# Scatter of expert rows by token, loads of 120 rows, and unread products between turned tiles

## The chip, the cores and the metric

The kernel runs on one core of one Trainium2 chip. The metric is the device time of one execution in microseconds (us). Kernels are compared by the median of several executions.

## The reference

The reference is a graph network of two layers over 1250 nodes with 768 features and 40,000 weighted edges. Layer 0 has two graph attention layers, linear attention and a mixture of experts, and its end is where the change lies. For each node a gate picks 2 of 8 experts. The node's row goes through both, and the two results are added with the gate's weights:

```python
h = jax.nn.relu(dispatched @ W1[e] + b1[e])
expert_outputs = expert_outputs + sel * (h @ W2[e] + b2[e])
...
rerouted = jnp.zeros((S * K, m), expert_outputs.dtype).at[dispatch_mask].set(expert_outputs)
combined = jnp.einsum('ks,ksm->sm', combine_weights, rerouted.reshape(K, S, m))
```

The combined rows are added to the residual and normalised (mean and variance over 768 features). Layer 1 begins with a low-rank adapter, relu(x Wd + bd) with 24 columns and then Wu, and a graph convolution with a 768x256 weight; linear attention and a spline layer follow. All of it is float32.

## The kernel before, in words

The nodes lie in 10 tiles of 125 rows. `acc` holds the residual, tile by tile, with a node to a partition. The order of instructions on each engine is written out by hand: each engine's program is a loop or a straight list, and semaphores tie them. PSUM is a ring of 4 slots of two banks, and `packets` is the list that says in which order the slots are taken. A slot is free once the packet 4 places earlier has been copied out.

Dispatch. A node's row of `xf` is scattered to two slots of `xs_rows` in HBM (POOL, indirect DMA), so that the rows of an expert lie together. SP then loads 27 tiles of 128 rows (`dispatched`, L654), and TensorE turns a tile (L1189), multiplies it by the expert's W1 (L1200) and W2 (L1211). VectorE copies the result to one of three buffers `yb` (L2309), and POOL writes it to `y_rows` in the same order of slots (L836).

Combine. When all of `y_rows` is written, POOL gathers for each tile of nodes 125 rows for the first expert and 125 for the second (L842, an indirect DMA each, 20 in all, into `back[k][t]`). For each tile VectorE adds share times row twice (L2328), then takes the statistics (L1832, L1834, L1835). ScalarE takes the root (L1417, `root_of`), VectorE the reciprocal and the negated mean times it (L2312, L2313, `lowered`), ScalarE writes the normalised tile to `H` (L1583, `normalised`). TensorE turns it with 6 transposes (L1238, packet `T x3`), and ScalarE copies the turned tile to `xT` (L1375, `turned_tile`).

Adapter. Its first product has two halves of the nodes, `down(0)` and `down(1)` (L955, packets `ad 0` and `ad 1`); ScalarE applies the relu (`low_rank`). `down(0)` stands after the seventh turned tile, `down(1)` after the tenth. Then TensorE forms the convolution's features (L1253, L1255, packets `cg`) and, with a weight that SP loads back from HBM when the tenth tile is normalised (`WA`, two loads at L551 from `spill_w`), the convolution itself (L1264).

## Time and profile before

| | |
|---|---|
| median of 3 runs | 2820.5 us |
| lowest, highest | 2816.82, 2822.02 us |
| the profiled execution | 2820.71 us |
| its span | 2819.0 us |
| mean granted clock of TensorE | 0.979 |
| PE busy | 2686.1 us (95%) |
| DVE busy | 1481.2 us (53%) |
| ACT busy | 889.0 us (32%) |
| POOL busy | 100.9 us (4%) |

The trace has PE for TensorE, PEld for its weight loads, DVE for VectorE, ACT for ScalarE, POOL for GpSimd, SP for the engine that issues most DMAs. Busy time says how much an engine ran, and not what ended a stage; for that the stretch between the last expert tile and the convolution has to be read alone. The expert loop runs from about 1195 to 1431 us of the span, the combine stage from 1431 to 1500 us, and `cg` begins at 1500.13 us.

### The profile page before, as it was taken

How to read it: one execution, taken by the hardware profiler on the slowest of the kernel's cores; microseconds unless marked ns; L12 is line 12 of the kernel's file. 1: busy time of each engine (PE TensorE's matmuls, PEld its weight loads, DVE VectorE, ACT ScalarE, POOL GpSimd, SP SyncE). 2: the span in 40 equal slices, each digit the busy share in tenths (PEclk: the TensorE clock that was granted, in tenths of full speed). 3: DMA queues.
4: the chain of work that ended last, by engine and by line, in shares of the span. 5: the costliest groups of instructions: out<-in, count | busy, mean ns of one | idle time of the engine just before them, and what ended most of it. 6: DMA issues, size and time to landing. Idle time of an engine off the chain costs nothing.

```text
span 2819.0 us, 30928 instructions
## 1 busy us (share of the span) xinstructions
PE 2686.1 (95%) x11845; PEld 1862.8 (66%) x11845; DVE 1481.2 (53%) x2298; ACT 889.0 (32%) x1528; POOL 100.9 (4%) x144
## 2 busy tenths in 40 slices
PE   6999999899989999899959999999999999999999
PEld 5786656698976556577736755566677776555555
DVE  7897899699962555511151210244877774331230
ACT  8895101244421332222221211032644442311210
POOL 1000000000000001100040000000000000000000
PEclk9999999999999999899969999999999999999999
DMA  9904222211030301499946111000200013000000
GB/s 236 334 5 92 96 65 70 72 72 38 19 72 28 73 12 53 139 386 359 358 138 136 39 34 34 0 15 1 90 30 30 30 34 130 6 11 6 11 11 11
DMA packets 131739, 238.12 MB, mean 84 GB/s; under 512 B 18639, under 2 KB 99572, under 8 KB 131118
## 3 DMA queue, kind: packets, MB, share of 16 engines
q1 hardware_dynamic: 116418, 192.97, 22.3%
q0 software_dynamic: 15200, 43.44, 4.6%
q8 instruction: 87, 1.43, 0.2%
q14 instruction: 34, 0.28, 0.0%
HBM read 173.10 MB, written 63.25 MB: 84 GB/s over the span
## 4 chain that ended last, share of the span: by engine, by line
PE 84%; DVE 9%; DMA 3%; ACT 1%; issue 1%; DVEq 1%; POOL 0%; SPq 0%; POOLq 0%; ACTq 0%
PE ps L938 22%; PE ps L1363 15%; PE ps L1320 14%; PE ps L1152 5%; PE ps L955 4%; PE ps L892 4%; PE ps L1062 4%; PE ps L1211 4%; PE ps L1200 4%; PE ps L1264 2%; DVE arena L1990 1%; DVE arena L1983 1%; DVE arena L1798 1%; PE ps L1253 1%; DMA arena<-in_x_dram 1%
## 5 line engine op out<-in xcount | busy, mean ns | idle before, releaser
L938 PE MATMUL ps<-arena 128*125 128x384 f32 x2112 | 697.1, 490 | 6.8 <-DVE arena L1909 2.7
L938 PEld LDWEIGHTS ps<-arena 128*125 128x125 f32 x2112 | 396.1, 189 | 284.3 <-issue 13.8
L1363 PE MATMUL ps<-arena 128*125 128x384 f32 x1280 | 415.4, 488 | 5.8 <-DVE arena L2395 5.8
L1320 PE MATMUL ps<-arena 128*128 128x312 f32 (+1 forms) x1536 | 407.1, 427 | 5.7 <-DVE arena L2395 5.7
L1320 PEld LDWEIGHTS ps<-arena 128*128 128x128 f32 x1536 | 291.6, 190 | 120.0 <-issue 6.6
L1363 PEld LDWEIGHTS ps<-arena 128*125 128x125 f32 x1280 | 241.3, 189 | 179.8 <-issue 8.5
L2395 DVE SCALAR_TENSOR_TENSOR arena<-arena 128x1250 f32<-128x1250 f32 (+3 forms) x175 | 232.0, 1347 | 93.9 <-PE ps L1320 91.6
L1375 ACT ACTIVATE arena<-ps 128x750 f32<-128x750 f32 (+6 forms) x140 | 108.1, 777 | 509.8 <-PE ps L938 201.2
L892 PE MATMUL ps<-arena 128*125 128x380 bf16 x1280 | 213.4, 328 | 11.1 <-DVE arena L1798 11.0
L1909 DVE SCALAR_TENSOR_TENSOR arena<-ps,arena 125x768 f32<-125x768 f32 x30 | 28.7, 955 | 346.9 <-PE ps L1363 292.9
L892 PEld LDWEIGHTS ps<-arena 128*125 128x125 bf16 x1280 | 173.0, 137 | 51.2 <-DVE arena L1798 14.0
L1391 ACT ACTIVATE arena<-arena 128x125 bf16<-128x125 bf16 x640 | 189.6, 386 | 34.0 <-DVE arena L1788 34.0
L1062 PE MATMUL ps<-arena 125*125 125x97 f32 x1600 | 179.0, 273 | 5.1 <-DVE arena L1990 5.1
L1062 PEld LDWEIGHTS ps<-arena 125*125 125x125 f32 x1600 | 177.7, 189 | 7.8 <-DVE arena L1990 4.2
L1968 DVE CUSTOM_DVE_ANT_0 arena<-arena 125x1250 bf16<-125x1250 bf16 x90 | 131.3, 1459 | 25.5 <-DMA arena<-al_src 22.9
L955 PE MATMUL ps<-arena 128*128 128x312 f32 (+5 forms) x496 | 138.1, 438 | 4.4 <-DVE arena L1938 2.4
L1152 PE MATMUL ps<-arena 125*125 125x385 f32 (+1 forms) x400 | 135.5, 494 | 2.8 <-DVE arena L2195 2.8
L2309 DVE COPY arena<-ps 128x768 f32<-128x768 f32 x27 | 25.8, 957 | 208.6 <-PE ps L1211 208.6
L1482 ACT ACTIVATE arena<-arena,small 125x1250 f32<-125x1250 f32 x80 | 105.2, 1333 | 71.3 <-DVE arena L1983 71.3
L1983 DVE SCALAR_TENSOR_TENSOR arena<-arena,small 125x1250 f32<-125x1250 f32 x80 | 120.8, 1512 | 2.8 <-DMA arena<-al_dst 2.8
L955 PEld LDWEIGHTS ps<-arena 128*128 128x128 f32 (+2 forms) x496 | 89.7, 183 | 47.7 <-issue 15.1
L1200 PEld LDWEIGHTS ps<-arena 128*128 128x128 f32 x972 | 112.7, 192 | 8.0 <-issue 1.2
(321 smaller groups left out, 2538.1 us busy)
## 6 DMA issues: line engine op xcount, KB each, us to landing
arena<-in_L_ffn_W_dram SPq DMA_DIRECT2D x54, 1152.0 KB, 7.8
xs_rows<-arena SPq DMA_DIRECT2D x1, 30720.0 KB, 99.5
arena<-in_kw_dram SPq DMA_DIRECT2D x24, 512.0 KB, 4.7
arena<-al_dst POOLq DMA_DIRECT2D x18, 625.0 KB, 4.9
arena<-xs_rows SPq DMA_DIRECT2D x27, 384.0 KB, 7.5
y_rows<-arena POOLq DMA_DIRECT2D x27, 384.0 KB, 6.5
arena<-in_kw_dram SPq DMA_DIRECT2D x6, 1536.0 KB, 10.0
arena<-in_x_dram SPq DMA_DIRECT2D x2, 3600.0 KB
```

Of the source, the lines that this page charges most:

```text
L892: mm = pe.matmul(bank(s, min(k, 1)), oh_src[:, par, u, k, :], oh_spot[:, par, u, :], start=(fresh and u == 0 and k < 2), stop=False, skip_ ...
L938: mm = pe.matmul(slot(g)[0:TILE, 512 * half:512 * half + HALF], xt[:, k, i * TILE:i * TILE + TILE], w[:, k, :], start=(k == 0), stop=(k == ...
L955: mm = pe.matmul(slot(g)[0:rows, 512 * b:512 * b + w], stat, mov[:, lo + b * w:lo + b * w + w], start=(t == 0), stop=(t == len(terms) - 1))
L1062: mm = pe.matmul(slot(g)[0:TILE, 512 * (j // 5) + 97 * (j % 5):512 * (j // 5) + 97 * (j % 5) + 97], AT[m % AHEAD][:, j * TILE:j * TILE + T ...
L1152: mm = pe.matmul(slot(g)[0:TILE, 512 * b:512 * b + w], AT2[i][:, j * TILE:j * TILE + TILE], H769[:, i, lo:lo + w], start=(i == 0), stop=(i ...
L1200: mm = pe.matmul(slot(g)[:, 0:TAU], w1s[t % ERING][:, k, f * P:f * P + P], xsT[t % 2][:, k, :], start=(k == 0), stop=(k == KT - 1))
L1320: mm = pe.matmul(slot(g)[:, 512 * b:512 * b + wd_], w[:, r % 2, ORDER[p], o * P:o * P + P], feat[place(f)][:, lo + b * wd_:lo + b * wd_ + ...
L1363: mm = pe.matmul(slot(g)[0:TILE, 512 * b:512 * b + HALF], fv[:, q, :], w2c[m][q][:, b * HALF:b * HALF + HALF], start=(p == 0 and q == 0), ...
L1391: ins = act.activation(oh_src[:, par, u, 1 + k, :], oh_src[:, par, u, 0, :], ACT.Copy, scale=w_p[k][:, bass.ds(col + u, 1)])
L1968: chain(dve.tensor_tensor_reduce(out=scratch, in0=neg[:, j, :], in1=row[0:TILE], scale=1.0, scalar=-3.0e38, op0=ALU.add, op1=ALU.max, accu ...
L1983: dve.scalar_tensor_tensor(out=AT[m % AHEAD], in0=d[0][0:TILE], scalar=alD[:, i, h:h + 1], in1=d[1][0:TILE], op0=ALU.add, op1=ALU.max).the ...
L2395: return dve.scalar_tensor_tensor(out=out_, in0=in_, scalar=edge, in1=of, op0=op, op1=ALU.mult)
```

## The change

The expert result now goes straight to its node, and several things follow from it.

1. A row of `xs_rows` has 770 words: the 768 features, the node's number plus one, and its first slot. The zero fill ahead covers 10,368 such rows. `slots` has one copy more.
2. In the expert loop VectorE works out, for each of the 128 rows of a tile, where its result belongs (`destination`, four small operations), and POOL scatters the tile by an indirect DMA to `z_rows`: rows 1 to 1250 the results for the first expert by node, the next 1250 those for the second, and spare rows behind. SP's load of tile t also waits until `destination` is done for tile t-3.
3. When all of `z_rows` is written, SP loads it: first rows 120 to 124 of all ten tiles, one load of 5 partitions for each expert (`back_rest`), then rows 0 to 119, 20 loads of 120 rows. The 20 gathers on POOL are gone.
4. VectorE's second addition gives the row's sum as well (`accum_out`). The squares are summed by ScalarE (`squares`, with the negated mean as bias), and VectorE's statistics are gone. The table for the root is loaded ahead (`primed`).
5. `low_rank(0)` stands behind the tenth turned tile instead of the seventh, and a tile is turned out one step later on ScalarE.
6. TensorE forms products of the identity with itself that nothing reads (`unread`): 40 behind the product for `F`, and 11 behind each of the first six turned tiles. Each set takes a slot of the ring.

```diff
+    packet("spin", NT)
     for i in range(NT):
         packet("T", "x3", i)
+        if i < 6:
+            packet("spin", i)
         if i == 6:
             packet("ad", 0)
...
+ROW = 768 + 2
+        xs_d = nc.dram_tensor("xs_rows", (EXP * ROOM + TAU, ROW), F32).ap()
+        z_d = nc.dram_tensor("z_rows", (1 + 2 * NODES + NTAU * TAU, D), F32).ap()
...
             def dispatched(t):
                 if t >= ERING:
                     sp.wait_ge(packet_ready, packets["sT", t - ERING] + 1)
+                    sp.wait_ge(ev("dest"), t - ERING + 1)
...
+            for q in range(3):
+                sp.wait_ge(ev(f"y_out{q}"), 16 * len(range(q, NTAU, 3)))
+            for k in range(2):
+                load(back_all[k][120:TILE], rows_z[k][120:TILE], "back_rest")
+            for t in range(NT):
+                for k in range(2):
+                    load(back[k][t][0:120], rows_z[k][0:120, t, :], f"back{t}")
...
             for n in range(NTAU):
                 emptied(pool, "so", n)
-                pool.dma_start(y_d[n * P:n * P + P], yb[n % 3]).then_inc(ev(f"y_out{n % 3}"), 16)
+                pool.wait_ge(ev("dest"), n + 1)
+                pool.indirect_dma_start(out=z_d, out_offset=bass.IndirectOffsetOnAxis(ap=desti[:, n:n + 1], axis=0),
+                                        in_=yb[n % 3], in_offset=None).then_inc(ev(f"y_out{n % 3}"), 16)
...
-                    pool.indirect_dma_start(out=back[k][t], out_offset=None, in_=y_d,
-                                            in_offset=bass.IndirectOffsetOnAxis(ap=ysloti[:, k, t:t + 1], axis=0))\
...
+            unread(NT, 40)
             for i in range(NT):
                 turn("x3", i, H)
                 if i == 6:
                     down(0)
+                elif i < 6:
+                    unread(i, 11)
             down(1)
...
+            def squares(i):
+                act.wait_ge(ev("centred"), i + 1)
+                act.activation(H[:, i, :], acc[:, i, :], ACT.Square, bias=nmu[:, i:i + 1], accum_out=ssq[:, i:i + 1])\
+                   .then_inc(ev("squared"), 1)
...
-            normalised(0)
-            for i in range(NT):
-                if i + 1 < NT:
-                    normalised(i + 1)
-                turned_tile("x3", i, xT)
-                if i == 6:
-                    act.wait_ge(ev("u_ones"), 1)
-                    low_rank(0)
+            own.step(act.activation(primed, onesc, ACT.Sqrt))
+            for i in range(NT):
+                squares(i)
+                root_of(i)
+                if i >= 1:
+                    turned_tile("x3", i - 1, xT)
+                normalised(i)
+            turned_tile("x3", NT - 1, xT)
+            act.wait_ge(ev("u_ones"), 1)
+            low_rank(0)
             low_rank(1)
...
+            def destination(n):
+                dve.wait_ge(ev(f"xs_{n % ERING}"), 16 * (n // ERING + 1))
+                own.step(dve.tensor_scalar(home[:, 0:1], first, rowp[:, n:n + 1], float(NODES), ALU.not_equal, ALU.mult))
+                chain(dve.tensor_scalar(home[:, 1:2], token, 0.0, spare[:, n:n + 1], ALU.is_equal, ALU.mult))
+                chain(dve.scalar_tensor_tensor(out=home[:, 0:1], in0=home[:, 0:1], scalar=home[:, 1:2], in1=token,
+                                               op0=ALU.add, op1=ALU.add))
+                dve.tensor_copy(desti[:, n:n + 1], home[:, 0:1]).then_inc(ev("dest"), 1)
...
+            dve.wait_ge(ev("back_rest"), 32)
             for t in range(NT):
                 dve.wait_ge(ev(f"back{t}"), 32)
...
+                own.step(dve.scalar_tensor_tensor(out=acc[:, t, :], in0=back[0][t], scalar=share[:, 0, t:t + 1],
+                                                  in1=acc[:, t, :], op0=ALU.mult, op1=ALU.add))
+                if t >= 1:
+                    varied(t - 1)
+                own.settle()
+                chain(dve.scalar_tensor_tensor(out=acc[:, t, :], in0=back[1][t], scalar=share[:, 1, t:t + 1],
+                                               in1=acc[:, t, :], op0=ALU.mult, op1=ALU.add, accum_out=total[:, t:t + 1]))
                 if t >= 1:
-                    lowered(t - 1, counted[t - 1])
+                    lowered(t - 1)
+                dve.tensor_scalar(nmu[:, t:t + 1], total[:, t:t + 1], -1.0 / D, None, ALU.mult).then_inc(ev("centred"), 1)
```

SP's list of DMAs, between the small weights of layer 1 and the return of `WA` (`spill_w`). Before:

```order
L551 DMA arena<-in_L_gnn_Wd_dram 128x6x24
L551 DMA arena<-in_L_gnn_Wu_dram 24x768
L551 DMA arena<-in_L_gnn_W_dram 128x6x256
L551 DMA small<-in_L_gnn_b_dram 125x256
L551 DMA arena<-spill_w 120x12800
L551 DMA arena<-spill_w 5x12800
```

and after the change, where `load` is L564:

```order
L564 DMA arena<-in_L_gnn_W_dram 128x6x256
L564 DMA small<-in_L_gnn_b_dram 125x256
L564 DMA arena<-z_rows 5x10x768 x2
L564 DMA arena<-z_rows 120x768 x20
L564 DMA arena<-spill_w 120x12800
L564 DMA arena<-spill_w 5x12800
```

The two loads of 5 partitions and the twenty of 120 rows stand in one queue, ahead of the return of `WA`.

TensorE's list from the product for `F` (25x256) to the first `cg`. Before:

```order
L1224 MATMUL ps<-arena 25x256 x6
L1238 MATMUL ps<-small,arena 128x125 x42
L955 MATMUL ps<-arena 24x312 x12
L1238 MATMUL ps<-small,arena 128x125 x18
L955 MATMUL ps<-arena 24x313 x12
L1253 MATMUL ps<-arena 125x256 x6
```

and after the change the head of the same place, where the turn is L1271 and the unread products L952 and L954:

```order
L1257 MATMUL ps<-arena 25x256 x6
L952 MATMUL ps<-small 128x128
L954 MATMUL ps<-small 128x128 x39
L1271 MATMUL ps<-small,arena 128x125 x6
L952 MATMUL ps<-small 128x128
L954 MATMUL ps<-small 128x128 x10
L1271 MATMUL ps<-small,arena 128x125 x6
```

The 42 transposes of the first seven tiles stood in one run; now 11 products stand between each two of them, and 40 ahead of the first. `down(0)` and `down(1)` keep their places.

ScalarE's list at the head of the combine stage. Before:

```order
L1417 ACT_TABLE_LOAD
L1417 ACTIVATE small<-small 125x1
L1583 ACTIVATE arena<-arena,small 125x768
L1417 ACTIVATE small<-small 125x1
L1583 ACTIVATE arena<-arena,small 125x768
L1375 ACTIVATE arena<-ps 128x6x125
```

and after, where the squares are L1618, the root L1453, the normalised tile L1623 and the copy of the turned tile L1411:

```order
L1626 ACTIVATE arena<-small 128x1
L1618 ACTIVATE arena<-arena 125x768
L1453 ACTIVATE small<-small 125x1
L1623 ACTIVATE arena<-arena,small 125x768
L1618 ACTIVATE arena<-arena 125x768
L1453 ACTIVATE small<-small 125x1
L1411 ACTIVATE arena<-ps 128x6x125
L1623 ACTIVATE arena<-arena,small 125x768
```

The copy of turned tile i now stands ahead of the normalising of tile i+1, and behind its squares and root.

## Rows read from the trace of the kernel before

**Rows 1.** Chain of waits, 1425 to 1450 us: start, us, what.
```profile
1430.42 2.59 DMA y_rows<-arena
...
1434.05 1.26 POOL arena L842
...
1435.61 7.80 DMA arena<-y_rows,arena
...
1443.44 1.03 DVE arena L2328
```

**Rows 2.** Timeline of TensorE, 1425 to 1545 us: start, us, what [idle before <-releaser].
```profile
1424.76 4.11 PE L1211 MATMUL ps<-arena 128*128 128x384 f32 x12 [0.66 <-ACT arena L1375]
...
1430.48 2.77 PE L1224 MATMUL ps<-arena 128*25 128x256 f32 x12 [1.13 <-DVE small L2321]
1451.84 1.51 PE L1238 MATMUL ps<-small,arena 125*128 125x125 f32 x6 [18.59 <-ACT arena L1583]
...
1474.24 1.51 PE L1238 MATMUL ps<-small,arena 125*128 125x125 f32 x6 [2.22 <-ACT arena L1583]
1475.69 8.44 PE L955 MATMUL ps<-arena 128*24 128x312 f32 x24
1484.06 0.86 PE L1238 MATMUL ps<-small,arena 125*128 125x125 f32 x6
...
1490.76 9.44 PE L955 MATMUL ps<-arena 128*24 128x313 f32 x24 [1.09 <-ACT arena L1375]
1500.13 2.85 PE L1253 MATMUL ps<-arena 128*125 128x256 f32 x12
...
1535.15 4.55 PE L1264 MATMUL ps<-arena 125*125 125x256 f32 x20
```

**Rows 3.** Timeline of VectorE, the second tile of the combine stage.
```profile
1449.01 1.02 DVE L1832 BATCH_NORM_STATS2 small<-arena 125x6 f32<-125x384 f32 x2
...
1450.57 0.16 DVE L2313 SCALAR_TENSOR_TENSOR arena<-small 125x1 f32<-125x1 f32 x1
```

**Rows 4.** Timeline of ScalarE in the combine stage.
```profile
1450.76 1.03 ACT L1583 ACTIVATE arena<-arena,small 125x768 f32<-125x768 f32 x1 [3.53 <-DVE arena L2313]
...
1455.43 0.78 ACT L1375 ACTIVATE arena<-ps 128x750 f32<-128x750 f32 x1
...
1484.23 0.77 ACT L1375 ACTIVATE arena<-ps,small 24x624 f32<-24x624 f32 x1 [5.63 <-PE ps L955]
```

**Rows 5.** ScalarE's read of a sum, line L1618: ns, first to last start.
```profile
L1618 ACT ACTIVATION_READ_ACCUMULATOR arena<-ps x20: 194/194/195, 1663.2 to 1893.4; 125x1 f32 x20
```

**Rows 6.** Windows: PE, PEld, DVE, ACT, POOL, PEclk, DMA share, GB/s.
```profile
820.00:823.00 3.00, 3.00 (x11) 1.77 (x10) 0.00 (x0) 0.00 (x0) 0.00 (x0) 1.00 0.98 194
...
825.00:826.00 1.00, 1.00 (x4) 0.56 (x3) 0.00 (x0) 0.00 (x0) 0.00 (x0) 1.00 0.92 69
...
1195.00:1431.00 236.00, 234.05 (x1431) 184.94 (x1431) 26.72 (x32) 51.52 (x107) 14.68 (x27) 1.00 0.95 341
...
1460.00:1470.00 10.00, 3.84 (x16) 2.67 (x15) 9.52 (x24) 4.20 (x8) 8.65 (x6) 0.50 0.70 210
```

**Rows 7.** VectorE's first read of x, in the timeline.
```profile
830.01 0.96 DVE L1909 SCALAR_TENSOR_TENSOR arena<-ps,arena 125x768 f32<-125x768 f32 x1 [11.12 <-DMA arena<-in_x_dram]
```

**Rows 8.** POOL's DMA queue, 1040 to 1150 us (14 scatters).
```profile
q0 software_dynamic: 3136, 5.39, 17.7%
```

**Rows 9.** POOL's DMA queue, 1195 to 1429 us (26 stores).
```profile
q0 software_dynamic: 2080, 10.23, 10.6%
```

**Rows 10.** Expert loop, a tile: SP's issue and TensorE's turn two tiles on.
```profile
1201.59 0.77 SPq L654 DMA_DIRECT2D arena<-xs_rows  x1
...
1221.85 0.82 PE L1189 MATMUL ps<-small,arena 128*128 128x128 f32 x6
```

**Rows 11.** DMA issues of the page: KB each, us to landing.
```profile
arena<-xs_rows SPq DMA_DIRECT2D x27, 384.0 KB, 7.5
```

**Rows 12.** SP's return of WA, in the timeline.
```profile
1488.79 0.69 SPq L551 DMA_DIRECT2D arena<-spill_w  x2
```

More of the change, by code:

```diff
@@ L395, in build @@
         sloti = rcut(2 * NT)[0:TILE].bitcast(I32).rearrange("p (k t) -> p k t", k=2)
-        yslotf = rcut(2 * NT)[0:TILE].rearrange("p (k t) -> p k t", k=2)
-        ysloti = rcut(2 * NT)[0:TILE].bitcast(I32).rearrange("p (k t) -> p k t", k=2)
+        total = rcut(NT)[0:TILE]
+        ssq = rcut(NT)[0:TILE]
+        nmu = rcut(NT)[0:TILE]
+        ptab = rcut(1)
+        spare = rcut(NTAU)
+        home = rcut(2)
+        primed = rcut(1)
         share = rcut(2 * NT)[0:TILE].rearrange("p (k t) -> p k t", k=2)
@@ L420, in build @@
         assert ro[0] <= 4700
-        xf = ct_r[0:TILE, 0:NT * D].rearrange("p (t d) -> p t d", t=NT)
+        X0 = R_ACC + R_XT + R_CT - NT * ROW
+        xf_all = arena[0:TILE, X0:X0 + NT * ROW].rearrange("p (t d) -> p t d", t=NT)
+        xf = [xf_all[:, NT - 1 - t, :] for t in range(NT)]
         xfT = [aa_r[:, 750 * n:750 * n + 750].rearrange("p (k n) -> p k n", k=KT) for n in range(2)]
@@ L424, in build @@
         w2s = [r[:, 2304:4608].rearrange("p (k n) -> p k n", k=3) for r in (aa_r[:, 0:4608], aa_r[:, 4608:9216], h_r)]
-        xs2 = [aa_r[:, 9216 + D * n:9984 + D * n] for n in range(ERING)]
+        xs2 = [aa_r[:, 9216 + ROW * n:9216 + ROW * n + ROW] for n in range(ERING)]
         xsT = [ct_r[:, D * n:D * n + D].rearrange("p (k n) -> p k n", k=KT) for n in range(2)]
@@ L824, in _ @@
             own.step(pool.memset(b2m, 0.0))
+            pool.wait_ge(ev("A_in"), (HEADS + 1) * NT)
+            own.step(pool.iota(ptab, [[0, 1]], base=0, channel_multiplier=1,
+                               allow_small_or_imprecise_dtypes=True))
+            own.step(pool.iota(spare, [[TAU, NTAU]], base=1 + NODES, channel_multiplier=1,
+                               allow_small_or_imprecise_dtypes=True))
+            own.step(pool.iota(xf_all[:, :, D], [[-TILE, NT]], base=1 + (NT - 1) * TILE, channel_multiplier=1,
+                               allow_small_or_imprecise_dtypes=True))
             own.settle()
@@ L922, in _, with unread @@
             pe.wait_ge(ev("adj_all"), 1)
+            def unread(n, times):
+                g = take_slot("spin", n)
+                pe.matmul(slot(g)[:, 0:P], ident, ident, start=True, stop=True).then_inc(slot_free[packet_at[g][0]], 1)
+                for _ in range(times - 1):
+                    mm = pe.matmul(slot(g)[:, 0:P], ident, ident, start=True, stop=True)
+                ready(mm)
             def transposes(s, src, event):
@@ L2257, in _ @@
                 emptied(dve, "agg2", j)
-                normal("xf", j, statistics(j, acc), acc, xf)
+                normal("xf", j, statistics(j, acc), acc, xf[j][:, 0:D])
             slots(NT - 2)
@@ L2291, in _ @@
                 chain(dve.tensor_reduce(b1t[:, :, f], btmp, AXX, ALU.add))
-            chain(dve.scalar_tensor_tensor(out=posf, in0=begin[0:TILE].unsqueeze(1).broadcast_to([TILE, NT, EXP]),
-                                           scalar=float(TAU), in1=pref, op0=ALU.mult, op1=ALU.add))
-            for k in range(2):
-                chain(dve.scalar_tensor_tensor(out=ptmp, in0=rank, scalar=float(k), in1=posf, op0=ALU.is_equal,
-                                               op1=ALU.mult))
-                chain(dve.tensor_reduce(yslotf[:, k, :], ptmp, AXX, ALU.add))
-            chain(dve.tensor_copy(ysloti, yslotf))
             dve.tensor_copy(rz, dinv).then_inc(ev("b1t"), 1)
@@ L2323, in _ @@
             give(dve.tensor_copy(WF, slot(g)[0:RANK + 1, 0:HID]), g)
-            counted = []
+            dve.wait_ge(ev("back_rest"), 32)
             for t in range(NT):
                 dve.wait_ge(ev(f"back{t}"), 32)
-                for k in range(2):
-                    chain(dve.scalar_tensor_tensor(out=acc[:, t, :], in0=back[k][t], scalar=share[:, k, t:t + 1],
-                                                   in1=acc[:, t, :], op0=ALU.mult, op1=ALU.add))
-                counted.append(statistics(t, acc))
+                own.step(dve.scalar_tensor_tensor(out=acc[:, t, :], in0=back[0][t], scalar=share[:, 0, t:t + 1],
+                                                  in1=acc[:, t, :], op0=ALU.mult, op1=ALU.add))
                 if t >= 1:
-                    lowered(t - 1, counted[t - 1])
-            lowered(NT - 1, counted[NT - 1])
+                    varied(t - 1)
[5 more added lines that the diff above has]
+                dve.tensor_scalar(nmu[:, t:t + 1], total[:, t:t + 1], -1.0 / D, None, ALU.mult).then_inc(ev("centred"), 1)
+                dve.wait_ge(ev("centred"), t + 1)
+            varied(NT - 1)
+            chain(dve.tensor_scalar(mv[:, :, 1], ssq, 1.0 / D, None, ALU.mult))
+            lowered(NT - 1)
             hs = rq
@@ L2434, in _ @@
                 emptied(dve, "vo", i)
[L2435 removed]
+                normal("x4", i, statistics(i, acc), acc, H[:, i, :])
                 if i == NT - 3:
```

54 lines of the change are left out of this document (30 added, 24 removed).

## The prediction

> **What bounds the kernel now.** I read the table of engines first, then the windows of the two stages that the change touches, then the chain of waits between them, then the three timelines of that stretch.
>
> In the expert loop TensorE runs 234.05 of 236 us and the DMA engines 0.95 of the time [rows 6]: TensorE sets the pace, with little room in the DMAs. Behind the loop nothing hides. The last expert product starts at 1424.76 [rows 2]; then come the last store (2.59 us), the issue of a gather on POOL (1.26), the first two gathers (7.80) and VectorE's first addition at 1443.44, which I call D0 [rows 1]. From there a tile costs what VectorE takes for two additions of 1.03 us [rows 1], 1.02 us of statistics and small operations of about 0.16 [rows 3]: turned tiles 0 and 6 begin at 1451.84 and 1474.24, so (1474.24 - 1451.84) / 6 = 3.73 us a tile. After T6 comes `down(0)`, 8.44 us, then T7 to T9, `down(1)`, 9.44 us, and `cg` at 1500.13 [rows 2]. Only four times on this path move: the loop's end, D0, T6 (now D0 + 30.8) and the tail from T6 to `cg` (now 25.9). The sum is made against the profiled execution of 2820.71 us (span 2819.0), which lies 0.2 us over the median of 2820.5.
>
> **The loop.** A tile takes 236/27 = 8.74 us. VectorE's and POOL's additions hide behind TensorE: four small operations are 4 x 0.16 = 0.6 us on an engine busy 26.72 of 236 us [rows 3, 6]. An xs load issued at 1201.59 is needed at 1221.85 and lands in 7.5 us [rows 10, 11], so 12.8 us are spare, and the new wait for `destination`, which I estimate at 2 us of delay, stays inside. What could not hide is DMA work. POOL's 14 indirect scatters of 125 rows took 17.7% of 110 us of 16 engines, 22.2 engine-us each [rows 8]; its 26 direct stores of 128 rows took 10.6% of 234 us, 15.3 each [rows 9]. The difference, 6.9 over 16 engines, is 0.43 us a tile. Used share 0.95 x 8.74 = 8.30, plus 0.43 is 8.73: just the pitch. Bounds 0 and 1.4 us for the loop; the copy added to each `slots` lies ahead of it. I take +0.2.
>
> **Last scatter.** A direct store took 2.59 us [rows 1], the gathers, also indirect, 7.80 for two. The scatter moves one tile, so I take 3.3, nearest the store: D0's first part is +0.7 (0 to 5.2).
>
> **The loads.** Gone are 1.26 + 7.80 us. New are a wait and an issue on SP, about 1.5 us, the two loads of 5 partitions, and the first two of 120 rows. The trace has both kinds once, in the load of x back as 120 rows and then 5. Its first part ran at 194 GB/s; from 825 us, when the 5 rows were left, it ran at 69, and went on until VectorE could read at 830.01 [rows 6, 7]. That is 5.1 us for 150 KB, with the engines' share still at 0.92. Both new loads go to the same 5 partitions, so I let them follow each other: 10.2 us. The first two loads of 120 rows are 737 KB, at 194 GB/s 3.8 us. They stand behind in the same queue. D0 = 1430.6 + 3.3 + 1.5 + 10.2 + 3.8 = 1449.4, against 1443.44: +6.0. Bounds: if the 5-row loads cost nothing beside the others, D0 is 1439.2; if the scatter takes its upper bound, 1453.9.
>
> The Trainium skill, "SBUF — State Buffer", section "Door 1: The DMA port swizzle (why `[64,N]` ≈ `[32,N]`)", has partitions 120 to 123 behind a single port of about 27 GB/s. By that rule the 123 KB of four of these rows would be an estimate of 4.5 us for each load; the trace, with 5.1 us, agrees. It speaks against this edit, since the wait for `back_rest` stands ahead of all tiles.
>
> **The pace.** The statistics leave VectorE, and a new circle forms through both engines: squares, their mean, the second addition of the next tile, reciprocal and scaled mean, normalising, next squares. With ScalarE at 0.94 for 125x768 (1.03 in its row less the overlap) [rows 4] plus 0.19 to read the sum [rows 5], that is 1.13 + 0.17 + 1.03 + 0.35 + 0.94 = 3.6 us. From D0 to T0 lie the first two additions and one such circle less the squares' wait, about 6.0 us, so T6 = D0 + 6.0 + 6 x 3.57 = D0 + 27.4 if the circle rules. Two loads a tile at 194 GB/s take 3.8; T6 needs the eighth pair (VectorE scales tile 6 behind the second addition of tile 7), so T6 = D0 + 7 x 3.8 + 3.6 = D0 + 30.2 if the data rule, and + 31.8 at 4.03 a pair. The products between turns are 22 records; `L1211` does a record of 384 columns in 4.11/12 = 0.34 us [rows 2], so one of 128 takes 0.11 at the upper clock, 2.5 for 22; with the turn (0.86) 3.3 us, under the pace. At the lower clock, granted from 1460 to 1470 at 0.50 [rows 6], it would be 1.51 + 4.9 = 6.4. The 40 products behind `F` (end 1433.25) last 9 us at the upper level and are over well before T0, so T0 finds the lower clock and T1 may be held by up to 2.8 us, made up by T6 but for at most 1.5. Between D0 + 27.4 and D0 + 31.8 I take D0 + 29.7: 1479.1, +4.9.
>
> **The tail.** If products keep the clock up, `down(0)` takes 24 records of 312 columns at 4.11/12 x 312/384 = 0.278: 6.7 us instead of 8.44, as in its own row it must have run at the lower level for part. No products stand behind T6, so `down(1)` stays near 9.3 (9.44). `low_rank(0)` (0.77) now comes behind the tenth turned tile, and its slot of the ring is the one `down(1)` needs: +0.8. Between them stand turned tiles, squares and normalising in series: 0.8 + 6.7 + 0.8 + 0.8 + 0.95 + 1.1 + 0.17 + 0.2 + 0.75 + 1.0 + 0.86 + 0.78 + 0.77 + 9.3 = 24.9, against 25.9: -1.0. The return of WA is issued behind the last normalised tile, before at 1488.79 [rows 12], 11.3 us ahead of `cg` and 46.4 ahead of its use at 1535.15 [rows 2]; both distances stay within 0.5 us, so nothing below moves.
>
> **Sum.** T6 +4.9, tail -1.0: `cg` at 1504.0, +3.9. 2820.71 + 3.9 gives 2824.6, about **2824.5 us**.
>
> **Rivals.**
> - *The 5-row loads are cheap.* They are small, and 120-row loads can pass on other engines meanwhile. D0 1439.2, T6 at D0 + 27.4 + 1.5, tail 24.9: `cg` at 1439.2 + 28.9 + 24.9 = 1493.0, 7.1 us earlier: 2813.6, faster. Against it stands the window at 69 GB/s [rows 6].
> - *Data and clock bind together* (slower). The loads share their HBM queue and SBUF side, and take 4.03 us a pair, so TensorE idles between the products and stays at the lower clock: T6 at 1449.4 + 0.5 + 31.8 = 1481.7, and `down(0)` at 8.44, tail 26.5, loop +1.4: `cg` at 1509.6, +9.5, 2830.2 us. It decides as soon as a pair of loads takes longer than the circle of 3.6 us. For it speaks that before, too, the engines were 0.70 busy at 210 GB/s while nothing waited for them [rows 6].
> - *The clock stays up through the tail*: `down(1)` at 6.7 instead of 9.3, T6 at D0 + 27.4: 2824.5 - 2.6 - 2.3 = 2819.6, no change.
> - *More rows per DMA engine.* The Trainium skill, "DMA: Bandwidth & Descriptors", section "Why a DMA increments its semaphore by 16 and not by 1", lets a load use as many engines, up to 16, as divide its slowest dimension: 15 for 120 rows, 5 for 125 or 5. By that rule the 120-row loads would run at 15/16 of the loop's rate; the 120-row part in the trace ran at 194 GB/s against the loop's 341. In rows, 737 KB at 320 GB/s would be 2.3 us a pair, D0 1447.9, pace 3.6, `cg` +0.6: 2821.3, no change.
>
> **Chances.** Forecast 0.44, of which 0.13 over the bound below; cheap 5-row loads 0.22, clock and data together 0.22, clock through the tail 0.07, faster 120-row loads 0.05. A measurement of this kernel tells 0.2%, 5.6 us, from no change: 2814.9 to 2826.1. Faster 0.22; slower 0.22 + 0.13 = 0.35; the rest, 0.43, no change. The likeliest case's own range is 2820 to 2828; that for 8 in 10 takes in both outer cases, 2811 to 2831.
>
> **What would show it.** Right: two loads of 5 partitions on the chain of waits, landing one after the other about 10 us behind SP's issue, D0 near 1449; pace 3.6 to 3.8; `down(0)` near 6.7 and `down(1)` near 9.3. If D0 is under 1443, the step on the 5-row loads is wrong; if the loop's end lies over 1432.5, that on the DMA room; if turned tiles come every 4 us with VectorE waiting for z_rows, the data rule and the slow rival holds; if they come so with TensorE never idle, it is the products. A changed distance between `cg` and the end would make the whole sum wrong.

## The result, and the profile after

| | before | after |
|---|---|---|
| median of 12 runs | 2819.72 us | 2814.57 us |
| lowest of them | 2816.54 us | 2810.53 us |
| the profiled execution | 2820.71 us | 2810.53 us |
| its span | 2819.0 us | 2808.8 us |

The ratio after to before is 0.9982, with a 95% interval of 0.9975 to 0.999: 0.18% faster, or 5.1 us, where the prediction had 3.9 us slower. That is less than the bound of 0.2%, but the interval excludes 1, so the sign is sure. Two executions in the whole record ran much longer at a lower clock, one of the kernel before (2907.26 us) and one of b_fill3072 (3109.77 us); they count in the medians and not in the ratios. The profiled execution of the changed kernel is the lowest of its twelve, so 10.2 us between the two profiles are more than the change is worth; where most of the other 5 come from is shown below.

The combine stage first, for it is what the prediction worked out. The chain of waits after, 1415 to 1490 us (start, us, what):

```profile
1418.26 0.97 DVE arena L2359
...
1419.81 3.00 DMA z_rows<-arena
...
1423.21 0.29 SPq L564
...
1425.39 15.35 DMA arena<-z_rows
1440.83 1.02 DVE arena L2383
...
1446.36 3.25 PE ps L954 x20
1449.60 0.66 PE ps L1271 x6
```

The last scatter took 3.00 us against 2.59 of the store. The chain then waits for SP's loads, and `1446.36 3.25` is a link that the chain of before has nothing like: unread products that hold the second turned tile. VectorE's timeline after (idle before in brackets) has the first addition and the pace:

```profile
1418.26 0.96 DVE L2359 COPY arena<-ps 128x768 f32<-128x768 f32 x1 [7.14 <-PE ps L1244]
...
1437.68 1.02 DVE L2383 SCALAR_TENSOR_TENSOR arena<-arena 125x768 f32<-125x768 f32 x1 [14.61 <-DMA arena<-z_rows]
...
1459.94 0.15 DVE L2362 TENSOR_SCALAR small<-arena 125x1 f32<-125x1 f32 x1 [0.90 <-ACT arena L1618]
...
1463.43 0.15 DVE L2362 TENSOR_SCALAR small<-arena 125x1 f32<-125x1 f32 x1 [0.90 <-ACT arena L1618]
```

From the last copy to the first addition are 19.4 us, where before it was 14.5. The first additions of the next tiles follow the loads, 3.15 us apart (1437.68, and 1440.83 in the chain above). After the delay of the second turned tile it is ScalarE's squares that VectorE waits for, 0.9 us in each tile, and a tile takes 3.49 us. The windows of the loads (the last three numbers: granted clock, DMA share, GB/s):

```profile
1426.00:1429.00 3.00, 3.00 (x29) 3.00 (x28) 0.00 (x0) 0.00 (x0) 0.00 (x0) 1.00 1.01 110
1429.00:1432.00 3.00, 2.74 (x25) 2.55 (x23) 0.00 (x0) 0.00 (x0) 0.00 (x0) 1.00 1.03 91
...
1441.00:1444.00 3.00, 0.00 (x0) 0.00 (x0) 2.31 (x8) 0.88 (x3) 0.00 (x0) 0.50 0.98 232
```

While the two loads of 5 partitions ran, the engines were busy throughout (share 1.01 to 1.03) and moved only 91 to 110 GB/s; afterwards the loads of 120 rows ran at 232, above the 194 of [rows 6]. The two windows, 6 us, hold about 600 KB, and the two small loads are 307 KB together, so some of the 120-row data moved beside them, slowly too. The trace's semaphore updates give the landings of the two small loads: the last part of the first at 1430.2 us, of the second at 1434.8. So they were served one after the other. TensorE's timeline after, to be laid beside [rows 2]:

```profile
1444.41 1.51 PE L1271 MATMUL ps<-small,arena 125*128 125x125 f32 x6 [12.67 <-ACT arena L1623]
...
1466.03 0.86 PE L1271 MATMUL ps<-small,arena 125*128 125x125 f32 x6 [0.18 <-ACT arena L1623]
1466.82 6.48 PE L988 MATMUL ps<-arena 128*24 128x312 f32 x24
...
1478.89 1.37 PE L1271 MATMUL ps<-small,arena 125*128 125x125 f32 x6 [2.15 <-ACT arena L1623]
1481.89 8.47 PE L988 MATMUL ps<-arena 128*24 128x313 f32 x24 [1.63 <-ACT arena L1411]
1490.28 2.86 PE L1289 MATMUL ps<-arena 128*125 128x256 f32 x12
```

`down(0)` runs wholly at the upper clock (6.48 us against 8.44 before), `down(1)` only in part (8.47). From the last copy to `cg` are 1490.28 - 1418.26 = 72.0 us, before 1500.13 - 1428.90 = 71.2: +0.8. From `cg` to the end of the span are 1318.5 against 1318.9. So in these two profiles the combine stage made the kernel slower by 0.8 us, and nearly everything gained was gained before the last copy of the expert loop, which came 10.6 us earlier. (More traces, further down, put the stage's loss nearer 1.6 us.)

Where it was gained is told by following the same TensorE line through both traces. Here is its first or last start before, in us, and the change after (minus is earlier):

| place in the program | start before | change after |
|---|---|---|
| adjacency from edges, first product | 26.4 | -0.2 |
| adjacency from edges, last product | 244.9 | -8.7 |
| first attention layer, last product | 810.2 | -7.5 |
| expert gate, first product (behind the second attention layer) | 1029.4 | -10.5 |
| experts, first turn | 1189.6 | -10.8 |
| `cg`, first product | 1500.1 | -9.8 |

8.5 us went in the very first stage, the building of the adjacency, in which no instruction of a compute engine is changed. Of what the change touches, only the zero fill of `xs_rows` runs beside it. The same window of 20 us in that stage, before:

```profile
60.00:80.00 20.00, 18.71 (x113) 14.76 (x112) 18.20 (x46) 16.62 (x57) 0.00 (x0) 1.00 1.01 354
```

and after:

```profile
60.00:80.00 20.00, 20.00 (x126) 16.91 (x125) 19.43 (x45) 18.14 (x62) 0.00 (x0) 1.00 1.07 238
```

TensorE had pauses there before and has none after; and the DMA engines, of which the fill is nearly all the work, moved 354 GB/s before and only 238 after. Once the fill of the kernel before is over, its TensorE has no pauses either:

```profile
140.00:160.00 20.00, 20.00 (x125) 16.37 (x124) 19.43 (x48) 18.14 (x63) 0.00 (x0) 1.00 0.09 30
```

The chain of waits of the kernel before goes through VectorE while the fill runs:

```profile
57.76 1.02 DVEq L1802
...
135.67 109.56 PE ps L892 x672
```

L1802 is the register load that tells VectorE in which columns of the adjacency a block lies. From 135.67 us, when the fill is over, TensorE sets the pace alone. The load's own rows before (ns, shortest, median and longest), first from 40 to 120 us with the fill, then from 210 to 240 us without:

```profile
L1802 DVEq TENSOR_LOAD <-arena x14: 314/1020/1040, 41.1 to 115.2; - x14
```

```profile
L1802 DVEq TENSOR_LOAD <-arena x6: 302/312/324, 211.5 to 237.5; - x6
```

The groups of VectorE's lines from 40 to 130 us show how much of that is not hidden, in the idle time before the first addition behind that load (last field). Before:

```profile
L1806 DVE TENSOR_TENSOR arena<-ps,arena 125x380 f32 x16 | 8.9, 554 | 6.2 <-issue 6.1
```

and after:

```profile
L1848 DVE TENSOR_TENSOR arena<-ps,arena 125x380 f32 x17 | 9.3, 547 | 0.3 <-issue 0.3
```

It is 6.2 us in 16 blocks, 0.39 us each, against 0.3 us in 17.

### The profile page after: what moved, and what is told of

It reads as the page before. It is cut to its first block, busy times and chain, and to the rows that moved or that the text cites. A ratio compares the mean times of both kernels' runs of the same rounds, so it can differ in the third digit from the quotient of the medians.

```text
span 2808.8 us, 31558 instructions
## 1 busy us (share of the span) xinstructions
PE 2703.9 (96%) x12057; PEld 1891.3 (67%) x12057; DVE 1487.0 (53%) x2402; ACT 899.6 (32%) x1549; POOL 83.4 (3%) x127
## 4 chain that ended last, share of the span: by engine, by line
PE 88%; DVE 6%; DMA 3%; ACT 2%; issue 1%; SPq 0%; POOL 0%; DVEq 0%; POOLq 0%; ACTq 0%
PE ps L971 22%; PE ps L1399 15%; PE ps L1356 14%; PE ps L917 7%; PE ps L1185 5%; PE ps L988 4%; PE ps L1095 4%; PE ps L1244 4%; PE ps L1233 4%; PE ps L1300 2%; DVE arena L2032 1%; DVE arena L2025 1%; PE ps L1289 1%; DMA arena<-in_x_dram 1%; PE ps L1316 1%; PE ps L1271 1%
## 5 line engine op out<-in xcount | busy, mean ns | idle before, releaser
L1411 ACT ACTIVATE arena<-ps 128x750 f32<-128x750 f32 (+6 forms) x140 | 108.2, 777 | 510.9 <-PE ps L971 194.7
L2010 DVE CUSTOM_DVE_ANT_0 arena<-arena 125x1250 bf16<-125x1250 bf16 x90 | 131.4, 1460 | 22.9 <-DMA arena<-al_src 20.3
L2359 DVE COPY arena<-ps 128x768 f32<-128x768 f32 x27 | 25.9, 958 | 191.8 <-PE ps L1244 191.8
```

Source lines behind the costliest of these rows:

```text
L2010: chain(dve.tensor_tensor_reduce(out=scratch, in0=neg[:, j, :], in1=row[0:TILE], scale=1.0, scalar=-3.0e38, op0=ALU.add, op1=ALU.max, accu ...
```

## The experiments

**The fill alone.** First comes the fill of the changed kernel in the kernel before, then the old pieces in the changed kernel, then other pieces in the kernel before.

```diff
-            load(xs_d.rearrange("(p q) (c n) -> p (q c) n", p=P, c=3),
-                 zero16.bitcast(F32).unsqueeze(1).broadcast_to([P, 3 * EXP * ROOM // P, 256]), "xs_zero")
+            load(xs_w.rearrange("(p q n) -> p q n", p=P, n=385),
+                 zero16.bitcast(F32)[:, 0:385].unsqueeze(1).broadcast_to([P, 2 * (EXP * ROOM + TAU) // P, 385]), "xs_zero")
```

> The kernel before with the fill exactly as the changed kernel has it: 10368 x 770 words in pieces of 1540 bytes, into a region of which the first part serves as xs_rows with rows of 768 words as before. Nothing else is changed. Theories A and B: the adjacency stage ends near 236 us instead of 245, and the whole is 5 to 9 us shorter than before, 2811 to 2815 us, so that the rest of the change is worth nothing or costs 1 us. Rival C: 2819 to 2821 us.

Measured: 2811.96 us, ratio to before 0.9974 (0.9965 to 0.9984), 6.8 us faster. The wait is gone:

```profile
L1807 DVE TENSOR_TENSOR arena<-ps,arena 125x380 f32 x17 | 9.3, 548 | 0.1
```

By the medians this one edit is worth more than the whole change. Rival C falls.

```diff
-            load(xs_d.rearrange("(p q) (c n) -> p (q c) n", p=P, c=2), ...
+            load(xs_w[0:P * 243 * 256].rearrange("(p q n) -> p q n", p=P, n=256), ...
+            load(xs_w[P * 243 * 256:].rearrange("(p n) -> p n", n=256), ...
```

> The changed kernel with one edit: the same 31.9 MB of zeros in pieces of 1024 bytes at multiples of 1024, as before the change. Theories A and B both expect the slow register loads back: adjacency stage to 244 or 245 us, time 5 to 9 us over the changed kernel, 2820 to 2823 us, that is 0 to 2 us over the kernel before. Rival C: stays at 2814 to 2815 us.

Measured: 2822.08 us, ratio 1.001 (1.0001 to 1.0018). The wait is back:

```profile
L1850 DVE TENSOR_TENSOR arena<-ps,arena 125x380 f32 x16 | 8.9, 554 | 6.0 <-issue 5.9
```

With the old pieces the change makes the kernel 3.3 us slower by the medians (0.3 to 5.1 by the interval). That is near the 3.9 that the prediction had worked out, though not all of its terms were right.

The next two ask what it is in the pieces (`c=2`, 384 words, and `c=1`, 768 words, in the fill of before).

> The kernel before with one edit: the zero fill of xs_rows in pieces of 1536 bytes (two a row) instead of 1024 (three a row). Theory A (it is the transfer rate: in the profile before the fill ran at 348 GB/s and VectorE's register load ahead of each block's additions took 1.03 us in the queue, in the changed kernel it ran at 245 GB/s and the wait was gone): aligned pieces of 1536 bytes run as fast as before or faster, the wait stays, the adjacency stage ends at 245 us, time 2819 to 2821 us. Theory B (it is the number of packets: 30720 against 20736): the wait goes, the stage ends near 237 us, time 2811 to 2815 us. Rival C (the gain ahead of the experts is not the fill at all): no change, and nothing changes in the other three runs either.

> The kernel before with the fill in pieces of 3072 bytes, one a row. Theory A (rate): the fill runs at 350 GB/s or more, the register load waits at least as long as before, 2819 to 2822 us. Theory B (number of packets, here 10240): the wait goes, 2811 to 2815 us. Rival C: 2819 to 2821 us.

Measured: 2819.6 us (interval of the ratio 0.9989 to 1.0007) for 1536 bytes, 2814.47 us (0.9974 to 0.9992) for 3072. The windows from 40 to 130 us, first of 1536 bytes, then of 3072:

```profile
40.00:130.00 90.00, 85.70 (x518) 69.07 (x517) 81.91 (x192) 75.81 (x257) 0.00 (x0) 1.00 1.00 369
```

```profile
40.00:130.00 90.00, 90.00 (x552) 73.89 (x551) 87.24 (x204) 80.49 (x272) 0.00 (x0) 1.00 0.99 383
```

Theory A (rate) falls with the second, theory B (the number of packets) with the first: the fill whose wait doesn't show is the faster one here, and 20480 pieces of 1536 bytes bring the wait while 20736 of 1540 don't. Left were packets per us, and alignment.

```diff
-                 ... n=385), ... [P, 2 * (EXP * ROOM + TAU) // P, 385]
+                 ... n=270), ... [P, 231, 270]          (1080 bytes)
+                 ... n=512), ... [P, 120, 512]          (2048 bytes, region of whole rows of 768)
```

> As b_fill1540, but with the 31.9 MB of zeros in pieces of 1080 bytes (29568 of them). After the first four runs two readings are left for why VectorE's register loads were slow with pieces of 1024 bytes (334 packets landed per us) and 1536 (237 per us) and not with 1540 (157) and 3072 (136). Theory D, packets per us: at the 245 GB/s of unaligned pieces this fill makes about 227 packets per us, so the wait of 0.37 us a block is back, the adjacency stage ends at 243 to 245 us, 2817 to 2820 us. Theory E, alignment and size both matter and unaligned pieces never disturb VectorE: stage ends at 236, 2811 to 2814 us.

> The kernel before with the fill in aligned pieces of 2048 bytes (15360). Theory D: at 370 to 380 GB/s about 183 packets per us, between 157 (no wait) and 237 (full wait): no wait or part of it, stage ends at 236 to 240 us, 2812 to 2816 us. Theory E: aligned pieces under 3072 bytes disturb: stage at 243 to 245, 2817 to 2820 us.

Measured: 2811.18 us (0.9962 to 0.9984) for 1080 bytes, 2818.79 us (0.9989 to 1.0008) for 2048. Theory D falls: 18765 packets from 40 to 130 us bring no wait, 16986 do.

```diff
+        xs_w = nc.dram_tensor("xs_rows", (EXP * ROOM * D + 1,), F32).ap()
+            load(xs_w[1:].rearrange("(p q n) -> p q n", p=P, n=384), ... [P, 160, 384]     (1536 bytes, one word on)
+            load(xs_w.rearrange("(p q n) -> p q n", p=P, n=1024), ... [P, 60, 1024]        (4096 bytes)
```

> As b_fill1536, pieces of 1536 bytes, but the region begins one word (4 bytes) further on, so that no piece begins at a multiple of 1024 or 512 bytes. Theory D (packets per us) has fallen: 2048-byte pieces at 189 packets per us gave the whole wait, 1080-byte pieces at 208 none. Theory E, what counts is alignment: the fill runs at 240 to 250 GB/s like the one of 1540, VectorE's register loads wait no longer, the adjacency stage ends at 236 us, 2811 to 2814 us. Rival (it is the odd piece length of 1540 and 1080, not where a piece begins): as b_fill1536, 370 GB/s, stage at 243, 2818 to 2820 us.

> The kernel before with the fill in aligned pieces of 4096 bytes. The fill of 3072 bytes ran at 383 GB/s without a wait. If long aligned pieces are as good as unaligned ones: stage ends at 236 us, 2811 to 2815 us. Rival (3072 was special, aligned powers of two disturb): stage at 243 to 245, 2817 to 2820 us.

Measured: 2811.72 us (0.9959 to 0.998) and 2812.64 us (0.9961 to 0.9983). The first makes the sharpest pair of all, for but for one more load of a single word it differs from b_fill1536 only in where a piece begins:

```profile
40.00:130.00 90.00, 90.00 (x558) 74.93 (x557) 86.92 (x206) 81.00 (x274) 0.00 (x0) 1.00 1.09 222
```

One word of shift takes the fill from 369 to 222 GB/s, fills TensorE's 90 us, and takes 8 us off the kernel. All fills together, each in the kernel before, from 40 to 130 us. "Aligned" means that every piece begins at a multiple of 512 bytes. Idle is that before the first addition, the register load is the median of its own rows from 40 to 120 us, and the stage ends with the last adjacency product:

| pieces, bytes | GB/s | packets | register load, ns | idle, us | stage ends, us |
|---|---|---|---|---|---|
| 1024 aligned (before) | 345 | 29799 | 1020 | 6.2 | 244.9 |
| 1536 aligned | 369 | 21376 | 1001 | 5.9 | 243.0 |
| 2048 aligned | 379 | 16986 | 1003 | 5.6 | 242.7 |
| 3072 aligned | 383 | 12263 | 583 | 0.3 | 236.5 |
| 4096 aligned | 384 | 9834 | 591 | 0.6 | 237.5 |
| 1080 | 231 | 18765 | 324 | 0.0 | 235.9 |
| 1540 (as after) | 247 | 14159 | 320 | 0.1 | 236.3 |
| 1536, one word on | 222 | 12730 | 319 | 0.6 | 236.1 |

The register load comes in three steps, and the whole times show only one of them. Without a fill it takes 0.31 us. Unaligned pieces leave it there (0.32), long aligned ones nearly double it, and aligned ones of up to 2048 bytes make it three times as long. The row of b_fill3072:

```profile
L1802 DVEq TENSOR_LOAD <-arena x16: 317/583/765, 39.7 to 119.7; - x16
```

At 0.58 us the load is still nearly all hidden behind the operations that VectorE has before it (idle 0.3 us in 17 blocks); at 1.0 us it no longer is. So the fill of 3072 bytes disturbs too, and only the slack in this stage hides it. Where the buffer of zeros lies in SBUF is not the cause: b_fill2048 and b_fill1536u both have one of 512 words, and stand at opposite ends. Why a shorter aligned piece lengthens the load more stays open: neither the rate, nor packets per us, nor the DMA engines' share (0.98 to 1.11 in all) orders the column.

**What the rest costs, on one chip.** The changed kernel and b_fill1540 were run again side by side, with no edit.

> The changed kernel again, beside the next three on one chip. Theory (the change is the fill's -7 us plus about +3 us for all the rest): 4 to 6 us under before, and 2 to 3 us over c_fill1540. Rival (the rest of the change costs nothing, and a_fill1024's 2822 us came from its own fill): within 1 us of c_fill1540.

> The kernel before with the changed kernel's zero fill, again, beside c_after. Theory: 6 to 8 us under before, 2 to 3 us under c_after.

Measured: 2814.46 us (0.9976 to 0.9994) and 2812.44 us (0.9967 to 0.9985). The difference is 2.0 us, and 2.6 us between the first runs of the two. Of the eleven executions of c_after eight lie above the highest of c_fill1540, 2813.5 us. With a_fill1024's 3.3 there are three measurements of the rest of the change, all slower, 2.0 to 3.3 us.

The two profiles at the start gave the combine stage only 0.8 us. The other traces say why: with its code unchanged the stage differs from one execution to the next. Here it is in all traces, in us:

| kernels (traces) | last copy to first addition | to the seventh turned tile | to `cg` | sum |
|---|---|---|---|---|
| before and the eight with only another fill (9) | 14.2 to 14.6 | 30.8 to 30.9 | 24.3 to 25.9 | 69.5 to 71.4 |
| after, c_after, a_fill1024 (3) | 19.2 to 19.4 | 28.4 to 28.5 | 24.3 | 72.0 to 72.2 |
| a_nospin, c_nospin (2) | 19.8 to 19.9 | 27.8 | 27.0 to 27.1 | 74.6 to 74.7 |
| a_norest | 10.3 | 29.4 | 24.9 | 64.5 |
| b_mix | 14.4 | 28.8 | 24.6 | 67.8 |
| c_mix_nospin | 14.0 | 27.8 | 26.0 | 67.9 |
| b_best | 14.3 | 29.2 | 21.2 | 64.8 |

In the first row the spread is in the tail: `down(0)` took 7.6 to 8.7 us there and `down(1)` 7.8 to 9.4. The kernel before had 71.2, near the top; the mean of its nine is 70.4. Against that the change costs the stage 1.6 us.

**The loads of 5 partitions.** They are left out here, so rows 120 to 124 of each tile are wrong: the run gives a price and is no version to use.

```diff
-            for k in range(2):
-                load(back_all[k][120:TILE], rows_z[k][120:TILE], "back_rest")
...
-            dve.wait_ge(ev("back_rest"), 32)
```

> The changed kernel without the two loads of 5 partitions, and without VectorE's wait for them; rows 120 to 124 of each tile of nodes are added from whatever the buffers hold. Everything else stands. Theory of the prediction (the two loads are served one after the other, about 5 us each, ahead of everything): the first addition starts 9 to 10 us earlier, cg 8 to 10 us earlier, 2805 to 2807 us. Rival (they overlap with the first pair of 120-row loads): 4 to 6 us earlier, 2809 to 2811 us.

Measured: 2803.48 us (0.9933 to 0.996), 11.1 us under the changed kernel and more than was expected; the profiled execution, 2806.86 us, is the slowest of its five. VectorE's timeline:

```profile
1421.70 0.96 DVE L2357 COPY arena<-ps 128x768 f32<-128x768 f32 x1 [7.14 <-PE ps L1242]
...
1431.95 1.02 DVE L2380 SCALAR_TENSOR_TENSOR arena<-arena 125x768 f32<-125x768 f32 x1 [5.45 <-DMA arena<-z_rows]
```

From last copy to first addition are 10.25 us instead of 19.4: the two loads cost 9.2 us, and the rival that they overlap with the first 120-row loads (4 to 6 us) falls. `cg` came 7.5 us earlier in its stage, not 9.2. Of the 1.7 us between, 1.1 were lost by the seventh turned tile, and TensorE's timeline says how:

```profile
1438.77 1.51 PE L1269 MATMUL ps<-small,arena 125*128 125x125 f32 x6 [3.60 <-ACT arena L1621]
...
1440.50 4.43 PE L952 MATMUL ps<-small 128*128 128x128 f32 x20
1444.77 0.81 PE L1269 MATMUL ps<-small,arena 125*128 125x125 f32 x6
```

The first products between the tiles run mostly at the lower clock (4.43 us, where later sets of 20 take 2.40) and hold the second turned tile for 2.5 us more than the pace of 3.49. The other 0.6 us came in the tail.

**The unread products.** The changed kernel without them, twice, and later b_mix without them:

```diff
-            unread(NT, 40)
             for i in range(NT):
                 turn("x3", i, H)
                 if i == 6:
                     down(0)
-                elif i < 6:
-                    unread(i, 11)
```

> The changed kernel without any unread product. Theory of the prediction: the clock stays at its lower level through the turned tiles, down(0) takes 8.4 us instead of 6.5, down(1) 9.4 instead of 8.5; the second turned tile is held no longer (0.7 us back). cg 2.2 us later, 2816.5 to 2817 us. Rival (the products buy nothing, since down(0) raises the clock itself): 2814 to 2815 us.

> The changed kernel without unread products, again, beside c_after. From the traces of the first run of each: cg 2.7 us later counted from the last expert product, so 2 to 3 us over c_after. Rival (the products pay back elsewhere what they save, as the first pair of times, 2814.9 and 2814.6, suggests): within 1 us of c_after.

Measured: 2814.86 us (0.997 to 0.9988), and 2815.65 us (0.9973 to 0.9991) beside c_after's 2814.46. TensorE's timeline of a_nospin:

```profile
1469.50 1.51 PE L1268 MATMUL ps<-small,arena 125*128 125x125 f32 x6 [1.98 <-ACT arena L1617]
1470.94 8.55 PE L985 MATMUL ps<-arena 128*24 128x312 f32 x24
...
1485.09 1.26 PE L1268 MATMUL ps<-small,arena 125*128 125x125 f32 x6 [2.15 <-ACT arena L1617]
```

`down(0)` is back at 8.55 us, and counted from the last copy `cg` comes 2.7 us later (2.5 in the second pair of traces). The whole times are less clear. The medians differ by 0.3 and 1.2 us, where 2 to 3 were expected, and the ratios to before come out the other way: 0.9979 and 0.9982 without the products, 0.9982 and 0.9985 with them. The executions without products spread from 2808.8 to 2817.6 us. So the gain of the stage is shown in two pairs of traces, and a gain of the whole kernel isn't.

**Gathers kept, the rest of the change in place.** The fill, the sums on ScalarE, the order of `low_rank(0)`, the early table and the products, with stores and gathers as before.

```diff
+            def squares(i): ...
+                elif i < 6:
+                    unread(i, 11)
                 pool.dma_start(y_d[n * P:n * P + P], yb[n % 3]).then_inc(ev(f"y_out{n % 3}"), 16)
...
                     pool.indirect_dma_start(out=back[k][t], out_offset=None, in_=y_d, ...
```

> The kernel before (stores and gathers by slot) with the fill of b_fill1540, and with the changed kernel's statistics on ScalarE, its order of low_rank, its early table load and its unread products. What is missing against the changed kernel is the scatter by node with its destinations and its loads. From the two profiles: last copy to first addition 14.5 us (before) instead of 19.4, first addition to seventh turned tile 28.4 instead of 30.8, from there to cg 24.3 instead of 25.9. So cg lies 4 us ahead of b_fill1540: 2812.0 - 4.0 = 2808.0 us, 6 to 7 us under the changed kernel. Rival: the gathers on POOL, of which each takes 1.4 us, or their data, set the pace at 3.7 us or more; then 2809.5 us or more.

> b_mix (gathers, ScalarE's sums of squares, the new fill) without its unread products. Theory: as in the changed kernel the products are worth 2 to 3 us: 2811 to 2812 us, within 1 us of c_fill1540, so that moving the statistics alone is worth about 1 us. Rival (products worth nothing): as b_mix, 2808 to 2809 us.

Measured: b_mix 2808.82 us (0.9953 to 0.9977), c_mix_nospin 2809.91 us (0.9951 to 0.9978). VectorE's timeline of b_mix:

```profile
1418.33 0.96 DVE L2334 COPY arena<-ps 128x768 f32<-128x768 f32 x1 [7.83 <-PE ps L1227]
...
1432.68 1.02 DVE L2357 SCALAR_TENSOR_TENSOR arena<-arena 125x768 f32<-125x768 f32 x1 [9.55 <-DMA arena<-y_rows,arena]
```

The gathers bring the first addition 14.4 us behind the copy, 5.1 ahead of the scatter and loads. POOL keeps up: from the sixth to the seventh turned tile are 3.49 us here too. So b_mix is 5.8 us faster than the changed kernel by the medians, where 6 to 7 were expected.

c_mix_nospin missed its expectation (2811 to 2812): the products bring b_mix 1.1 us by the medians and nothing in the stage of the two traces, 67.8 and 67.9 us. What they save in the tail (24.6 against 26.0) they lose before the seventh turned tile (28.8 against 27.8). Between c_mix_nospin and c_fill1540 stand the sums on ScalarE, the early table and the order of `low_rank(0)`: 2.5 us by the medians where 1 was expected, 1.7 in the stage of the two traces. The intervals of the ratios overlap, so the size is not sure.

**A version that beats both.**

```diff
-            turned_tile("x3", NT - 1, xT)
             act.wait_ge(ev("u_ones"), 1)
             low_rank(0)
+            turned_tile("x3", NT - 1, xT)
...
                 g = take_slot("T", s, i)
+                for _ in range(7 if s == "x3" and i > 7 else 0):
+                    pe.matmul(slot(g)[:, 0:P], ident, ident, start=True, stop=True)
                 pe.wait_ge(ev("ln_" + s), i + 1)
```

> b_mix with two edits: low_rank(0) ahead of the copy of the tenth turned tile, where ScalarE waits for TensorE anyway (0.7 us off the path), and 7 unread products each ahead of the ninth and the tenth turned tile, in their own slot of PSUM, so that the clock is at its upper level for the tenth turn (0.86 instead of 1.51) and for down(1) (6.5 instead of 8.7). From b_mix's profile: cg 0.7 + 0.6 + 2.2 = 3.5 us earlier, 2808.8 - 3.5 = 2805.3 us. Rival (the wait of 1.6 us before down(1) lets the clock fall all the same): only 0.7 to 1.3 us, 2807.5 to 2808 us.

Measured: 2805.4 us, ratio 0.9947 (0.9933 to 0.9961), 14.4 us under before. TensorE's timeline:

```profile
1477.53 0.86 PE L1256 MATMUL ps<-small,arena 125*128 125x125 f32 x6 [0.58 <-ACT arena L1608]
1479.48 6.48 PE L971 MATMUL ps<-arena 128*24 128x313 f32 x24 [1.08 <-ACT arena L1396]
1485.89 2.85 PE L1274 MATMUL ps<-arena 128*125 128x256 f32 x12
```

The tenth turn (0.86 us) and `down(1)` (6.48) run at the upper clock, as expected. The two edits were not tried apart; together they give 3.4 us against b_mix by the medians.

**The other 5 us of the profiled execution.** Between 913 and 1029 us, in the second attention layer, the profiled execution of the changed kernel gained 6.0 us on before, that of b_fill1540 1.9, that of b_mix 3.4, that of a_nospin lost 0.4. A window there of before, then of after:

```profile
995.00:1015.00 20.00, 17.16 (x49) 9.48 (x48) 14.16 (x7) 6.84 (x6) 1.91 (x3) 0.91 0.03 3
```

```profile
995.00:1015.00 20.00, 19.41 (x60) 11.28 (x61) 12.36 (x13) 0.20 (x1) 0.46 (x4) 1.00 0.01 2
```

Before, the mean granted clock of this window is 0.91 of full speed; after, in this execution, it is 1.00. It comes and goes between kernels that are alike there (0.91 in a_norest, 1.00 in b_mix), and between executions of one kernel: c_after, which is the changed kernel again, has

```profile
995.00:1015.00 20.00, 20.00 (x55) 11.23 (x54) 11.13 (x12) 0.20 (x1) 0.00 (x0) 0.86 0.01 2
```

and gained 0.8 us between 913 and 1029 us, not 6.0. So it is the execution and not the change, and it explains most of why the profiles differ by 10.2 us and the medians by 5.1.

## Why the prediction was wrong

The step that failed is the sentence "Only four times on this path move", with the sum that it opens: all stages ahead of the expert loop were put at nothing without a reason. The change list of the document itself names a fifth thing, a zero fill of 10,368 rows, and the prediction gives it no term. Its new piece length, 1540 bytes instead of 1024, is a by-product of rows of 770 words. In b_fill1540 it takes 8.6 us off the adjacency stage and 6.8 off the kernel, by way of VectorE's register load. That outweighs the loss of 2.0 to 3.3 us by everything else in the change, whose sign the prediction had right.

The terms that were worked out, each against the changed kernel's profile:

| term | forecast, us | measured, us |
|---|---|---|
| loop, from its first turn to its last product | +0.2 | +0.1 |
| last scatter | 3.3 | 3.0 |
| last copy to first addition | 20.3 | 19.4 |
| first addition to seventh turned tile | 29.7 | 28.35 |
| seventh turned tile to `cg` | 24.9 | 24.25 |
| combine stage against before | +3.7 | +0.8 |
| `cg` to the end | 0 | -0.4 |

- The loads of 5 partitions: right in kind, served one after the other; a_norest puts 9.2 us on them where the prediction had 10.2. The estimate in the prediction by the Trainium skill, "SBUF — State Buffer", section "Door 1: The DMA port swizzle (why `[64,N]` ≈ `[32,N]`)", is 4.5 us for each. It is nearer than the 5.1 us that the prediction read from the load of x and used.
- The loads of 120 rows: mis-sized. A pair took 3.15 us and not 3.8, for it ran at 232 GB/s and not at the 194 of the one row that was read. So the circle through both engines ruled the later tiles, as one of the two bounds had it: 3.6 us forecast, 3.49 measured. The rival of faster 120-row loads, 2.3 us a pair, went too far.
- The products: as forecast they held the second turned tile, which came 5.03 us behind the first, and most of that was made up by the seventh. `down(0)` took 6.48 us (forecast 6.7), `down(1)` 8.47 (forecast 9.3).
- The first rival (cheap 5-row loads) forecast a faster kernel, 2813.6 us, for a reason that the traces refute: its first addition should have come 4.2 us earlier than before (1439.2 against 1443.44), and counted from the last copy it came 4.9 us later. That the time came out near it is luck, the fill's doing. It is luck too that 2814.57 lies inside the wide range of 2811 to 2831, for that end stood for the cheap loads.
- The stage's sum was high by 2.9 us against the profile before: 0.9 in the first addition, 1.35 in the pace and 0.65 in the tail. Against whole times, 2.0 to 3.3 us for all but the fill, the sum of 3.9 was high by one or two.
- The 14 terms of the tail add up to 25.0 and not 24.9; that changes nothing.

## What to carry to other kernels

Go through the diff for transfers that run in the background and change shape or alignment, not only for edits on the path, and give each a term: here a fill that nobody waits for slowed another engine's register loads for as long as it ran, nearly 100 us. A change that bundles several ideas is to be split before it is kept: the scatter by node and its loads cost more than the gathers they replace, and without them the kernel is 6 us faster. When a small load of few partitions stands ahead of a wait, take its price from how long such a load took in a trace, and not from its bytes at the rate of a wide load. A stage whose code is untouched can still differ by 2 us between traces, so read it in more than one before a difference of 1 us is believed.

## What was not expected of the hardware

- A fill from one SBUF buffer to HBM lengthens VectorE's register load. It takes 0.31 us without a fill, 1.00 to 1.02 us beside aligned pieces of 1024, 1536 or 2048 bytes, 0.58 to 0.59 beside aligned pieces of 3072 or 4096, and 0.32 beside pieces that begin off alignment. In this stage only the longest of these shows, as 0.35 to 0.39 us of idle time a block.
- Moving the start of 1536-byte pieces by 4 bytes lowers their rate from 369 to 222 GB/s.
- Two loads of 5 partitions and 150 KB each cost 9.2 us, and while they ran the loads behind them in the queue were slow too: 91 to 110 GB/s with the DMA engines' share at 1.01 to 1.03, against 232 at 0.98 afterwards.
- The granted clock dips in the second attention layer in some executions and not in others of the same code (1.00 in after, 0.86 in c_after, from 995 to 1015 us). Between 913 and 1029 us the profiled executions named above differ by up to 6.4 us; a profile taken alone would have made the change twice as good as it is.
